# Mixture-of-experts results placed by matrix products: four of eight experts in two float32r parts instead of three in three bf16 parts

## What is computed

```
xe = zeros((E, CAP, d)).at[se, pos].set(xf[tok], mode='drop')        # E = 64 experts, CAP = 128 slots each
h = silu(einsum('ecd,edi->eci', xe, gate_proj)) * einsum('ecd,edi->eci', xe, up_proj)
ye = einsum('eci,eid->ecd', h, down_proj)
contrib = where(valid, ye[se, posc], 0.0) * flat_w[order]
out = zeros((m, d)).at[tok].add(contrib)                             # each token is the sum of 8 experts' rows
```

## Time and profile before

| What | Value |
|---|---|
| median of 3 runs | 410.79 us (410.63 to 410.82) |
| the profiled execution's own time | 411.59 us |
| its span | 409.8 us, mean granted clock of PE 0.928 |
| PE busy | 335.7 us, 82% |
| POOL busy | 260.6 us, 64% |
| DVE busy | 305.5 us, 75% |
| ACT busy | 258.2 us, 63% |
| expert steps | about 235 us to 390 us of the span |

### The profile page before, as it was taken

The page is one execution under the profiler, slowest core; times in us unless marked ns, Lnnn a source line. Parts: engine busy times, 40 slices in busy tenths (PEclk is TensorE's granted clock), DMA queues, the critical chain, the costliest instruction groups (busy, mean ns, idle before and its releaser), DMA issues.

```text
span 409.8 us, 7559 instructions
## 1 busy us (share of the span) xinstructions
PE 335.7 (82%) x2206; PEld 269.0 (66%) x2217; DVE 305.5 (75%) x694; ACT 258.2 (63%) x528; POOL 260.6 (64%) x213
## 2 busy tenths in 40 slices
PE   4948944697798799799893299999999998999980
PEld 2433733365566567567793287998999897998960
DVE  2999999899999999999998937445453544454365
ACT  0998989999888888987265354445444443544410
POOL 4200041789978878887514678778878778787830
PEclk9997875799999989999899589999999999999995
DMA  8930520666435777331396349899888998865466
GB/s 233 375 123 14 155 102 0 219 229 220 155 114 186 258 264 251 129 136 51 85 268 175 112 103 247 204 230 225 214 217 213 233 224 194 215 146 91 84 123 226
DMA packets 59132, 72.17 MB, mean 176 GB/s; under 512 B 6802, under 2 KB 43458, under 8 KB 59106
## 3 DMA queue, kind: packets, MB, share of 16 engines
q1 hardware_dynamic: 49104, 56.04, 43.8%
q0 software_dynamic: 8832, 15.74, 19.2%
q10 hardware_dynamic: 1170, 0.08, 0.2%
HBM read 61.75 MB, written 10.09 MB: 175 GB/s over the span
## 4 chain that ended last, share of the span: by engine, by line
PE 43%; ACT 20%; DVE 15%; DMA 10%; issue 7%; POOL 2%; SPq 0%; DVEq 0%; POOLq 0%; ACTq 0%
PE bank L1319 12%; PE bank L1357 9%; PE bank L1312 5%; ACT ssm L853 4%; PE bank L1299 3%; DVE bank L1556 3%; ACT L853 3%; DMA ssm<-routed,idx 3%; ACT L891 3%; DVE ssm L1561 2%; DMA ssm<-bc_rows 2%; PE bank L1153 2%; DMA du<-sums 2%; DMA B_last<-bc_rows 2%; PE bank L1065 2%
## 5 line engine op out<-in xcount | busy, mean ns | idle before, releaser
L602 POOL TENSOR_TENSOR ssm<-ssm,arena 128x1024 f32<-128x1024 f32 x31 | 73.1, 2358 | 18.5 <-issue 10.2
L1561 DVE TENSOR_TENSOR_SCAN ssm<-ssm,bank 128x512 f32<-128x512 f32 x64 | 78.1, 1221 | 4.0 <-issue 1.8
L675 POOL DMA_INDIRECT ssm<-routed,idx x64 | 65.2, 1019 | 21.8 <-issue 14.6
L1784 DVE SCALAR_TENSOR_TENSOR ssm<-ssm,bank 128x96 f32<-128x96 f32 x64 | 20.0, 313 | 75.9 <-ACT ssm L965 75.7
L686 POOL DMA_INDIRECT sums<-ssm,idx x40 | 65.6, 1639 | 13.9 <-issue 10.4
L1319 PE MATMUL bank<-ssm,wguT 128*128 128x256 bf16 x576 | 72.4, 272 | 0.3 <-DVE ssm L1776 0.3
L1319 PEld LDWEIGHTS bank<-ssm,wguT 128*128 128x128 bf16 x576 | 56.0, 97 | 12.3 <-DVE ssm L1776 0.6
L965 ACT ACTIVATE ssm<-bank 128x96 f32<-128x96 f32 x64 | 16.0, 250 | 74.1 <-PE bank L1357 74.1
L1357 PE MATMUL bank<-arena,ssm 128*128 (+1 forms) x256 | 53.3, 331 | 1.6 <-ACT ssm L948 1.1
L1153 PE MATMUL bank<-xs,wguT 128*128 128x512 bf16 x182 | 44.4, 393 | 11.1 <-POOL xs L589 4.6
L853 ACT ACTIVATE ssm<-delta,A_sb 128x510 f32<-128x510 f32 x64 | 43.9, 713 | 6.8 <-DVE ssm L1561 6.7
(11 more groups left out here) (225 smaller groups left out, 663.7 us busy)
## 6 DMA issues: line engine op xcount, KB each, us to landing
ssm<-bc_rows SPq DMA_DIRECT2D x22, 512.0 KB, 3.7
arena<-bc_rows SPq DMA_DIRECT2D x16, 512.0 KB, 4.9
arena<-in_L_ffn_gate_proj SPq DMA_DIRECT2D x32, 192.0 KB
arena<-in_L_ffn_up_proj SPq DMA_DIRECT2D x32, 192.0 KB
arena<-in_L_ffn_down_proj SPq DMA_DIRECT2D x32, 192.0 KB
B_last<-bc_rows SPq DMA_DIRECT2D x10, 512.0 KB, 3.6
sums<-zero_f SPq DMA_DIRECT2D x1, 2304.0 KB, 14.1
arena<-in_L_ffn_w_gate_up SPq DMA_DIRECT2D x1, 2048.0 KB, 11.4
```

The source lines that it names most:

```text
L602: pool.tensor_tensor(prod[:, a:b, :], hs[:, a:b, :], C_all[:, 2 * (q % 8):2 * (q % 8) + 2, :], ALU.mult).then_inc(s.prod_ok, 1)
L675: pool.indirect_dma_start(out=xe[:, k, :], out_offset=None, in_=routed, in_offset=bass.IndirectOffsetOnAxis(ap=idx2[:, k, 0:1], axis=0)).t ...
L1561: dve.tensor_tensor_scan(hs[:, k % 4, :], dA[:, k % 3, :], x[:, :], 0.0, ALU.mult, ALU.add).then_inc(s.scan_ok, 1)
```

## The change

`ON_PE` becomes (1, 3, 5, 7): 32 of 64 experts are placed by PE (24 before) and 32 scattered (40 before). The 0/1 tiles and the parts are float32r, a float32 whose reduced-precision form TensorE takes as it stands, and there are two parts: `hi` = the rows as float32r, `lo` = rows - `hi`. That is 16 products per placed expert, 64 a round, 8 in every step. Placing of an expert begins four experts later (`PLACED_LATE`) on DVE, in the odd steps, and five on PE. `places` and `ye_parts` lie in double buffers over dead feed-forward tensors. The scattered experts are now the even ones, each always on the same plane of `sums`. In the first round the zeroing of bank 7 comes ahead of that step's placing.

```diff
@@ -46,7 +47,8 @@
 NACC = 2
-ON_PE = (1, 4, 7)
+ON_PE = (1, 3, 5, 7)
+PLACED_LATE = 4
@@ -350,9 +354,8 @@
         token = part(xin[:, 0, 0, 0:1], (1, TOK // 2)).bitcast(F16)
-        places = part(wguT[:, 0, 0:1], (1, 3 * TOK)).rearrange("p (b j m) -> p b j m", b=3, m=P)
-        ye_parts = part(ssm_flat, (1, 9 * D // 2), offset=6656).bitcast(BF16).rearrange("p (b c d) -> p b c d", b=3, d=D)
-        ye_rest = part(ssm_flat, (1, D), offset=7808)
+        places = nc.alloc_sbuf_tensor_at("places", [P, 2, NT, P], F32R, offset=at_wgu).ap()
+        ye_parts = nc.alloc_sbuf_tensor_at("ye_parts", [P, 2, 2, D], F32R, offset=at_ffn).ap()
@@ -515,9 +518,8 @@
             for a in range(NACC):
-                for n, k in enumerate(others):
-                    last = (ROUNDS - 1 + n) % 2 == a
-                    sp.wait_ge(m_scatter[k], 16 * (ROUNDS if last else ROUNDS - 1))
+                for k in others[a::NACC]:
+                    sp.wait_ge(m_scatter[k], 16 * ROUNDS)
@@ -550,10 +552,9 @@
             for k in range(NX):
-                first = others.index(k) % 2 if k in others else 0
-                step = 0 if k in ON_PE else -AROWS if first else AROWS
-                pool.iota(part(sum_base[:, 0:1], (2 * NX, ROUNDS // 2), (NX, 2), offset=k), [[0, ROUNDS // 2], [step, 2]],
-                          base=AROWS * first, channel_multiplier=0, allow_small_or_imprecise_dtypes=True).then_inc(s.c_ident, 1)
+                plane = others.index(k) % NACC if k in others else 0
+                pool.iota(part(sum_base[:, 0:1], (NX, ROUNDS), offset=k), [[0, ROUNDS]],
+                          base=AROWS * plane, channel_multiplier=0, allow_small_or_imprecise_dtypes=True).then_inc(s.c_ident, 1)
@@ -1311,36 +1312,22 @@
 
-            def place(*parts):
-
-                for which, tiles in parts:
-                    for j in tiles:
-                        for c in range(3):
-                            ins = pe.matmul(bank[4 + j // 2][:, (j % 2) * D:(j % 2) * D + D], places[:, which, j, :], ye_parts[:, which, c, :],
-                                            start=False, stop=False, skip_group_check=True)
+            def place(b, tiles):
+
+                for j in tiles:
+                    for c in range(2):
+                        ins = pe.matmul(bank[4 + j // 2][:, (j % 2) * D:(j % 2) * D + D], places[:, b, j, :], ye_parts[:, b, c, :],
+                                        start=False, stop=False, skip_group_check=True)
                 ins.then_inc(s.m_placed, 1)
 
             def place_of_step(k, i):
 
-                if k == 6:
-                    pe.wait_ge(s.m_oh, i * 15 + 6)
...
+                b = (k // 2 + 1) % 2
+                if k % 2 == 0:
+                    pe.wait_ge(s.m_oh, i * 12 + (3 * k // 2 - 5))
+                    place(b, range(4))
                 else:
+                    place(b, range(4, 8))
@@ -1372,16 +1359,15 @@
                         zero((4, 5, 6))
+                    if first and k == 7:
+                        pe.wait_ge(s.idx_step, 6)
+                        zero((7,))
                     if not (first and k < 6):
                         place_of_step(k, i)
                     if first and k == 6:
                         by_slot(1)
-                    if first and k == 7:
-                        pe.wait_ge(s.idx_step, 6)
-                        zero((7,))
 
             turn_input(0, 16)
-            pe.sem_inc(s.m_placed, 6)
@@ -1389,12 +1375,13 @@
             down(NX - 1, RING - 1, E - 1)
-            pe.wait_ge(s.m_oh, ROUNDS * 15 - 4)
-            place((0, (6, 7)))
-            place((1, range(NT)))
-            pe.wait_ge(s.m_oh, ROUNDS * 15 + 1)
+            for k in range(2):
+                place_of_step(k, ROUNDS)
+            pe.wait_ge(s.m_oh, 1 + 3 * E // 2 - 3)
+            place(0, range(8))
+            pe.wait_ge(s.m_oh, 1 + 3 * E // 2)
             for q in range(4):
-                place((2, (2 * q, 2 * q + 1)))
+                place(1, (2 * q, 2 * q + 1))
@@ -1759,21 +1746,17 @@
 
-            def places_of(which, e):
-
-                dve.tensor_scalar(places[:, which, :, :].rearrange("p j m -> p (j m)"), token, part(fix[:, 0:1], (1, 1), offset=e), None,
+            def places_of(b, e):
+
+                dve.tensor_scalar(places[:, b, :, :].rearrange("p j m -> p (j m)"), token, part(fix[:, 0:1], (1, 1), offset=e), None,
                                   ALU.is_equal).then_inc(s.m_oh, 1)
 
-            def three_parts(which, count):
-
-                y, hi, mid, lo = ye[:, ON_PE[which], :], ye_parts[:, which, 0, :], ye_parts[:, which, 1, :], ye_parts[:, which, 2, :]
+            def two_parts(b, k, count):
+
+                y, hi, lo = ye[:, k, :], ye_parts[:, b, 0, :], ye_parts[:, b, 1, :]
                 dve.tensor_copy(hi, y).then_inc(s.m_oh, 1)
-                dve.wait_ge(s.m_oh, count + 1)
-                dve.tensor_tensor(ye_rest, y, hi, ALU.subtract).then_inc(s.m_oh, 1)
                 dve.wait_ge(s.m_oh, count + 2)
-                dve.tensor_copy(mid, ye_rest).then_inc(s.m_oh, 1)
-                dve.wait_ge(s.m_oh, count + 3)
-                dve.tensor_tensor(lo, ye_rest, mid, ALU.subtract).then_inc(s.m_oh, 1)
+                dve.tensor_tensor(lo, y, hi, ALU.subtract).then_inc(s.m_oh, 1)
@@ -1787,31 +1770,19 @@
                     dve.tensor_copy(idx2[:, k, 1:2], row_i[:, bass.ds(e, 1)]).then_inc(s.idx_ok, 1)
-                    if k == 0 and not first:
-                        dve.wait_ge(s.m_placed, i * 8 - 2)
-                        places_of(2, e - 1)
...
                     if first and k in (4, 5, 6):
                         diagonals(1, (k - 4,))
                     if first and k == 7:
                         rows(1)
-                    if k == 7:
-                        dve.wait_ge(s.m_ye, i * 8 + 6)
-                        three_parts(1, i * 15 + 7)
+                    if k % 2 == 1 and not (first and k < 5):
+                        if first:
+                            dve.wait_ge(s.m_oh, 1)
+                        else:
+                            dve.wait_ge(s.m_placed, i * 8 + (k - 7))
+                        b = ((k - 5) // 2) % 2
+                        places_of(b, e - PLACED_LATE)
+                        dve.wait_ge(s.m_ye, e - 2)
+                        two_parts(b, (k - PLACED_LATE) % NX, i * 12 + (3 * k - 15) // 2 + 1)
@@ -1823,13 +1794,17 @@
 
-            dve.wait_ge(s.m_placed, ROUNDS * 8 - 2)
-            places_of(2, E - 1)
-            dve.wait_ge(s.m_ye, ROUNDS * 8 + 1)
-            three_parts(2, ROUNDS * 15 - 3)
+            dve.wait_ge(s.m_placed, E - 6)
+            places_of(0, E - 3)
+            dve.wait_ge(s.m_ye, E - 1)
+            two_parts(0, NX - 3, 1 + 3 * (E // 2 - 2))
+            dve.wait_ge(s.m_placed, E - 4)
+            places_of(1, E - 1)
+            dve.wait_ge(s.m_ye, E + 1)
+            two_parts(1, NX - 1, 1 + 3 * (E // 2 - 1))
             for q in range(4):
                 t = slice(2 * q, 2 * q + 2)
-                dve.wait_ge(s.m_placed, ROUNDS * 8 + 3 + q)
+                dve.wait_ge(s.m_placed, E - 2 + q)
```

More of the change, by code:

```diff
@@ L21 @@
 F16 = mybir.dt.float16
+F32R = mybir.dt.float32r
 I16 = mybir.dt.int16
@@ L258, in build @@
         x2T = ssm[:, 3]
+        at_wgu = nc.sbuf_base
         wguT = sb("wguT", [P, 2, 2 * H], BF16)
         wpT = sb("wpT", [P, HC, D])
+        at_ffn = nc.sbuf_base
         ffn = sb("ffn", [P, 6, 512])
@@ L1312, in down @@
                 pe.matmul(of_result(), hhT[0:I, k % 2, :], w_dn[:, bass.ds(slot, 1), :], start=True, stop=True).then_inc(s.m_y_ps, 1)
-            def place(*parts):
-                for which, tiles in parts:
-                    for j in tiles:
-                        for c in range(3):
-                            ins = pe.matmul(bank[4 + j // 2][:, (j % 2) * D:(j % 2) * D + D], places[:, which, j, :], ye_parts[:, which, c, :],
-                                            start=False, stop=False, skip_group_check=True)
+            def place(b, tiles):
[3 more added lines that the diff above has]
+                                        start=False, stop=False, skip_group_check=True)
                 ins.then_inc(s.m_placed, 1)
             def place_of_step(k, i):
-                if k == 6:
-                    pe.wait_ge(s.m_oh, i * 15 + 6)
-                    place((0, (0, 1, 2)))
-                elif k == 7:
-                    place((0, (3, 4, 5)))
-                elif k == 0:
-                    pe.wait_ge(s.m_oh, i * 15 - 4)
-                    place((0, (6, 7)), (1, (0,)))
-                elif k == 1:
-                    place((1, (1, 2, 3)))
-                elif k == 2:
-                    place((1, (4, 5, 6)))
-                elif k == 3:
-                    pe.wait_ge(s.m_oh, i * 15 + 1)
-                    place((1, (7,)), (2, (0, 1)))
-                elif k == 4:
-                    place((2, (2, 3, 4)))
+                b = (k // 2 + 1) % 2
+                if k % 2 == 0:
```

(22 more changed lines are left out.)

## The result

| | before | changed kernel |
|---|---|---|
| median of 4 runs | 410.81 us (410.63 to 412.10) | 406.43 us (406.17 to 407.29) |
| ratio | | 0.9894, 95% interval 0.9859 to 0.9928 |
| profiled execution | 411.59 us, span 409.8 | 407.29 us, span 405.5 |
| mean granted clock of PE | 0.928 | 0.923 |

Faster by 4.4 us. The forecast was 9.3 us faster: the direction came, and less than half of the size. 406.43 lies at the very edge of the range (399 to 406.5).

What follows compares the result with a forecast made beforehand. PE was taken to bound the experts' stretch, POOL just behind. Steps and waits 7.5 us, first round 0.3 and end 1.5 sum to 9.3 less: 401.5 us against the median, range 399 to 406.5.

Steps and rivals of the forecast that it cites:

- PE's pace: Placing products on PE: eight float32r ones at 110 ns each, 0.88 us for 0.98, a step of 2.31 for 2.41.
- The count of one pass: Each float32r placing product streams its 256 columns in one pass, 109 ns, where true float32 takes four passes.
- the rival of 215 ns: Half-pace stream: each float32r placing product takes 215 ns, step 3.15, time about 450 us; chance 0.12.
- The load of 108: Weight load of 128 float32 columns on PE takes 108 ns and must hide behind a product of 109.
- The waits for gathers: Between experts 9 and 63, PE's two waits for gathered inputs, 2.1 us together, go because POOL no longer falls behind.
- The first round: First round of experts: shorter DVE splitting lets expert 9's product start earlier; 0.3 us less, bounds -0.3 to 0.8.
- The end: After the last experts: first plane loaded 2.2 us earlier, second 0.35 earlier; 1.5 us less taken.
- The part on PE's end: PE's last 48 products at 110 ns end some 1 us before the 54 did; DVE's sums are not late.
- DVE: DVE in odd steps: tiles at 0.81 us, work of 2.0 us hidden with 0.5 to spare, cost nothing.
- DVE late: Rival: tiles take 1.28 us or the cast is held up, PE waits in odd steps; 407 to 409.5, chance 0.06.
- DMA full: Rival: weights or gathers set the pace until the last weights are in, 38 steps gain nothing; 405.3 us, chance 0.05.
- POOL: POOL's round of gathers and scatters falls from 20.1 to 18.2 us against PE's 18.5, so it keeps up.

Runs made afterwards that it cites:

- fp16 kernel: The changed kernel with the 0/1 tiles and the two parts in float16 in place of float32r, nothing else; 400.48 us, ratio 0.9771.

## Why the prediction was right in sign and wrong in size

- **The step that failed** is PE's pace, "I take 110". It measured 120. Then 8 x 0.120 = 0.96, and with the 0.11 of the hidden transpose the placing needs 1.07 us for 1.09 before. The step became 2.38, not 2.31. Against the forecast's own 2.41 these 54 steps bring 1.6 us and not 5.4: 3.8 of the 4.9 us that are missing. The fp16 kernel, whose products keep 109, has the step of 2.30, and with half the weights, 512 or 128 columns the step follows the products' pace (2.347, 2.353, 2.317) without a wait for a gather. The worst pace that the prediction's range allowed for was 113.
- **Why I took it.** The count of one pass was right: the rival of 215 ns is out, by a factor. It was worked out from the Trainium skill (FP8 and Floating Point Precision, TensorE Precision Notes), which has four passes for true float32 alone and gives no pace for the reduced form. The load of 108 was nearly right (112). What I leaned on for the two together was the row of eight float32 transposes at 110. These have 128 moving columns. With 128 columns the float32r products also keep 112, the pace of the load alone. The row thus shows what a load costs behind a product that needn't be as long as it, and not what it costs when both want 110 ns. No row of before had both at that size, and the honest bounds for it were 109 and 217, with a lean above the lower end. The rule of the Trainium skill (TensorE: Matmul & The Clock Gate, Weight-path perf modes) that a float32 tile has no fast load was the warning. By the 107 ns of the Trainium skill's formula (TensorE: Matmul & The Clock Gate, LDWEIGHTS) the load was as long as the product, and the runs come near it with 112. I noted it and then priced it at 1 ns.
- **The waits for gathers** went, as forecast. But the 2.1 us that they were priced at stood in one profile; in two others they are 1.0 and 0.7. Some 1.1 to 1.4 us of the forecast was this execution's own, though it stood 0.8 us over the median, which I had seen.
- **The first round**: 0.3 forecast, 0.3 from the two profiles first compared; against the others 0.4 to 1.4. Not settled to better than that.
- **The end**: 1.5 forecast, 1.9 measured there (21.3 to 19.4), and 1.2 to 1.4 against the two other profiles. Its inner working was right for the first plane (2.2 forecast, 2.0 measured) and the second (0.35 and 0.2). What I had not seen is that the loads, 3.8 us apart and no longer side by side, both bring their pieces before DVE wants them. The part on PE's end was wrong: counted from expert 63, its last 48 products end 0.2 us earlier and not 1 (9.84 for 10.01), and DVE's first sum starts 0.36 later (8.44 for 8.08).
- **DVE**: tiles 0.81 forecast, 0.75 measured; no wait of PE for them. The rival "DVE late" is out, as is "DMA full" (the share fell to 0.86, and no wait for weights).
- **POOL**: no waits for gathers, but less idle than I reckoned, since its transfers grew by 5 to 7%. At the forecast step of 2.31 a round of 19.1 us would have put POOL 0.6 us behind PE in each. Before, 0.8 us a round came out as 0.7 to 2.1 us of waits in all, so this would have cost up to some 1.6 us, by my estimate. Whether the transfers would have grown as much there, no run shows, because in the fp16 kernel they hardly grew.
- **The sum** by measured terms: 1.6 for the steps, 2.1 for the waits, 0.3 for the first round, 1.9 for the end are 5.9 us from the profiled 174.9 to 169.0. Against the other two profiles of before it is 4 to 5, which agrees with the 4.4 of the medians.
- **The range**: that 406.43 lies inside it is luck. Its slow end of 406.5 was made for transfers that fill the DMA engines and for a late DVE, and neither came. The sign, too, owes less to the term that was to carry it (5.4 forecast for the steps, 1.6 measured) than to the smaller ones.

## What to carry to other kernels

Fewer matrix products are a gain only by their pace, and a pace comes from a row where stream and weight load have the sizes they will have: when the load is about as long as the product that hides it, don't price the meeting of the two at nothing. If a reduced type is wanted for its bits, try the 16-bit type that nearly has them as well: here two fp16 parts give more than twice what two float32r parts give. And where two engines are nearly level, take from both in one change; what is taken from one alone comes back as a wait.

## What the runs showed of the hardware

- A float32r product of 128x128 weights takes 120 ns for 256 moving columns at the full granted clock, where a 16-bit one takes 109: 113 in a long series when the load is halved or when 512 columns go in one product (227), 112 when only 128 columns are streamed. A 4-byte type is thus not slower by half or more, and not free either.
- POOL's indirect transfers of the same size took longer in both profiles of the changed kernel than in the three of the kernel before, from 260 to 380 us: gathers 1041 and 1049 ns for 994 to 1001, scatters 1755 and 1759 for 1621 to 1638. The DMA share was lower meanwhile (0.78 and 0.79 for 0.84 and 0.85, from 265 to 380 us) and the traffic about the same (199 and 204 GB/s for 200 and 201). Extra 4-byte writes by DVE did not bring it about. The cause is open.
- The part before the experts, which the change leaves as it is, took from 234.8 to 239.6 us in the profiles, more than the whole effect under study. A stretch between two marks inside the same profile told the change from it; the span did not.
